# Layer 1's attention: half of the loads of the last keys' values issued one tile later, and the third bank's exponentials after the fourth query product

## What is computed

```python
x = x + tanh(g_xattn[0]) * L0_xattn(layernorm(x), ctx)      # 16 heads of 16
x = x + tanh(g_ffn[0])   * L0_ffn(layernorm(x))             # mixture of 8 experts, tokens 0..1023
x = x + tanh(g_xattn[1]) * L1_xattn(layernorm(x), ctx)      # 16 heads of 64, 77 keys
x = x + tanh(g_ffn[1])   * L1_ffn(x)                        # 32 prototypes, the two nearest, rank 16
```

```python
q = x @ Wq / 8 ; logits = q k^T ; w = softmax(logits) ; ctx = w v ; y = x + gate * ctx @ Wo
dist to 32 prototypes -> two nearest, weights wt ; y += gate * sum_t wt * (A[idx] @ (B[idx] @ y) + bias[idx])
```

## Time and profile before

| | |
|---|---|
| runs shown | 3024.16, 3027.03, 3029.62 us; median 3027.03 |
| profiled execution | 3032.24 us, with a span of 3030.5 us |
| granted TensorE clock over the span | 0.97 |
| busy share of the span | PE 91%, DVE 81%, ACT 73%, POOL 69% |
| stage of layer 1 | from about 1450 us to the end |
| its bodies 4 to 15, 16 to 47, 48 to 61 | 1547 to 1837, 1837 to 2595, 2595 to 2920 us |

### The profile page before, as it was taken

How to read it: one execution, slowest core, us unless ns; L and a number is a source line. 1 busy time by engine, 2 the same in 40 slices (tenths; PEclk the granted TensorE clock), 3 DMA queues, 4 the chain that set the end, 5 groups by cost and what they waited for, 6 DMA issues and landing times. The chain is left out here.

```text
span 3030.5 us, 96782 instructions
## 1 busy us (share of the span) xinstructions
PE 2744.3 (91%) x31534; PEld 2165.7 (71%) x31534; DVE 2452.0 (81%) x5870; ACT 2202.5 (73%) x5452; POOL 2090.0 (69%) x2777
## 2 busy tenths in 40 slices
PE   3889896899999999789699999999999999999996
PEld 2444444677777777557588878888878888888884
DVE  6888786688888888675588898888888888888884
ACT  2666666677787777575577777788777788778873
POOL 3893000566667666554478888888888888888886
PEclk7999999899999999899899999999999999999998
DMA  5997666223323233632467677777767777777763
GB/s 152 352 346 292 244 255 254 78 77 91 84 80 93 77 90 85 219 111 48 110 142 157 150 153 150 145 147 144 145 139 152 147 146 145 155 148 149 151 132 75
DMA packets 636894, 455.53 MB, mean 150 GB/s; under 512 B 387712, under 2 KB 610544, under 8 KB 631600
## 3 DMA queue, kind: packets, MB, share of 16 engines
q1 hardware_dynamic: 616240, 402.30, 53.7%
q0 software_dynamic: 7328, 23.40, 2.5%
q10 hardware_dynamic: 12960, 25.23, 2.3%
HBM read 235.08 MB, written 148.83 MB: 127 GB/s over the span
## 5 line engine op out<-in xcount | busy, mean ns | idle before, releaser
L383 POOL TENSOR_TENSOR a_probT_lo<-a_expT,a_probT_hi 128x512 f16<-128x512 f32 x256 | 291.4, 1159 | 217.7 <-ACT a_probT_hi L466 217.7
L459 ACT ACTIVATE a_expT<-banks,a_top,w_score_scale 128x512 f32<-128x512 f32 (+1 forms) x384 | 272.6, 710 | 152.8 <-PE banks L550 145.3
L1160 POOL TENSOR_TENSOR a_pn<-a_prob,a_rsum 128x1024 f32<-128x1024 f32 (+1 forms) x256 | 310.6, 1235 | 54.1 <-DVE a_rsum L1541 54.0
L1242 ACT ACTIVATE a_qT_hi<-banks 128x512 f16<-128x512 f32 x252 | 151.2, 600 | 212.3 <-PE banks L152 212.3
L150 PE MATMUL banks<-a_xnT,w_q_hi 128*128 128x256 f16 x1024 | 280.6, 274 | 15.4 <-DMA a_xnT<-a_xn_parts 13.5
L150 PE MATMUL banks<-a_vo_front,a_probT_hi 128*128 128x256 f16 x1024 | 279.9, 273 | 9.0 <-DVE a_probT_lo L1527 3.5
L1525 DVE TENSOR_TENSOR a_qT_lo<-banks,a_qT_hi 128x512 f16<-128x512 f32 x252 | 172.4, 684 | 141.6 <-ACT a_qT_hi L1242 141.6
L151 PE MATMUL banks<-a_xnT,w_q_hi 128*128 128x256 f16 x1024 | 280.3, 274 | 0.0
L152 PE MATMUL banks<-a_xnT,w_q_lo 128*128 128x256 f16 x1024 | 280.2, 274 | 0.0
L152 PE MATMUL banks<-a_vo_front,a_probT_lo 128*128 128x256 f16 x1024 | 279.9, 273 | 0.0
L151 PE MATMUL banks<-a_vo_front,a_probT_hi 128*128 128x256 f16 x1024 | 279.8, 273 | 0.0
(11 more groups left out here) (383 smaller groups left out, 10323.8 us busy)
## 6 DMA issues: line engine op xcount, KB each, us to landing
vo<-kv_vo_out SPq DMA_DIRECT2D x38, 2048.0 KB, 7.4
a_vo_front<-vo SPq DMA_DIRECT2D x128, 512.0 KB
kt<-kv_k_out ACTq DMA_DIRECT2D x9, 2560.0 KB, 15.0
a_k<-kt SPq DMA_DIRECT2D x64, 308.0 KB, 3.9
kv_raw_e<-in_L_ffn_w POOLq DMA_DIRECT2D x16, 1024.0 KB, 9.7
a_x<-in_x SPq DMA_DIRECT2D x64, 256.0 KB
a_y<-in_x SPq DMA_DIRECT2D x64, 256.0 KB, 2.8
x<-a_y SPq DMA_DIRECT2D x64, 256.0 KB, 3.0
```

Source lines behind the costliest of these rows:

```text
L383: pool.tensor_tensor(probT[b][1][:, first:end, :], expT[b][:, first:end, :], probT[b][0][:, first:end, :], ALU.subtract).then_inc(prob_rea ...
L459: act.activation(expT[1 - h][0:rows, first:end, :], bank, ACT.Exp, bias=top[0:rows, 0:1], scale=weights["score_scale"][0:rows, 0:1]).then_ ...
L1160: last = pool.tensor_tensor(keys_of(pn[h]), e[:, :, first:end], rsum[h][:, :].unsqueeze(2).broadcast_to([P, H, end - first]), ALU.mult)
L1242: act.activation(out, bank[:, 0:cols].rearrange("p (c s) -> p c s", c=out.shape[1]), ACT.Copy, scale=scale)\
```

## The change

`load_values` gets a range of the eight `vo_back` loads. In half 0 SP issues the two `vo_front` loads and the first four `vo_back` loads; in half 1, after the store of the output, it issues the other four. They then stand ahead of the next body's keys and `xnT`. And in ScalarE's list `prep(4)`, the high part of the fourth query product, comes ahead of `third_exponentials`; `prep(4)` has work in half 1 alone.

```diff
-        def load_values(i, u, j):
+        def load_values(i, u, j, first, end):
             p, _ = turn(u, j, 2)
             need(sp, y_ready, (i - 1) * TPB)
-            for a in range(2):
+            for a in range(2 if first == 0 else 0):
                 sp.dma_start(vo_front[p][a * FRONT:(a + 1) * FRONT, :, :, :], values_front(batch_at(i), a)).then_inc(vo_in[p], 16)
-            for n in range(MAIN):
+            for n in range(first, end):
                 sp.dma_start(vo_back[p][n * BACK:(n + 1) * BACK, :, :, :], values_back(batch_at(i), n)).then_inc(vo_in[p], 16)
...
-                if h == 0 and live(i, NB):
-                    load_values(i, u, j)
+                if live(i, NB):
+                    load_values(i, u, j, *((0, MAIN // 2), (MAIN // 2, MAIN))[h])
...
+                prep(4)
                 if live(t, NT):
                     third_exponentials(t, u, h)
-                prep(4)
                 prep(2)
```

## The result

The changed kernel takes 3105.5 us (median of 4 runs, 3101.4 to 3110.0) against 3028.3 us for the kernel before (4 runs). The ratio is 1.026, with a 95% interval of 1.025 to 1.028: slower by 77 us, where 31 were forecast, and outside the range given. The profiled execution took 3101.4 us with a span of 3099.7, 69.2 us more than before. The 77 us are the difference of the medians; the profiled execution before lay 4 us above its median, and this one was the fastest of its four.

A forecast was written before the change was run, and what follows sets the result against it. The prediction took TensorE's list to bound the kernel. Its terms, 29 + 9 + 1 - 8 - 0 = 31 us, put the time at 3058 us by the median of 3027.0, with a range of 3022 to 3080.

The forecast's parts named there:

- What bounds the kernel: TensorE's list sets the time; the change can win only from its idle pieces, 32.0 + 8.9 us and 17.0 us.
- Part 1, what it relieves: With four loads instead of eight on SP, `hwT` goes out when ready, 2.9 us earlier; gain 8 us, bounds 0 and 12.7.
- The term of 8 us: Gain taken in the loop's bodies from `hwT` going out when ready; bounds 0 and 12.7 us.
- Part 1, what it delays: Four loads ahead of the next body's `xnT` make TensorE wait: 29 us loop, 1 us last stretch, 9 us first stretch.
- the loop's sum: In the loop `xnT` is issued about 2009.9, lands at 2013.9, wanted at 2012.87; 0.9 us wait taken, 29 us in 32 bodies.
- 1 us in all: Last stretch: wait for `xnT` of 0.1 us in 14 bodies, bounds 0 and 14 us.
- The first stretch's 9 us: Wait for `xnT` of 1.5 us in six bodies with the experts' rows, 9 us, bounds 3 and 14.
- A landing of 4.8 us everywhere: Rival, 0.08: small loads slow the transpose; waits of 32 x 1.8 + 14 + 14 = 86 us, less 8: 3105 us.
- Part 2: ScalarE exchange: VectorE's stall moves to a wait for `attend`, `a_pick` still ends with GpSimd's L1167; 0 us, otherwise 9 us.
- the transpose lands in time: Rival, 0.12: at the first query product TensorE never waits for `xnT`; 3019 us, or 3014 with 12.7 us won.
- delay and gain even out: Rival, 0.07: waits of 0.1 to 0.4 us in the loop and 3 us in the first stretch, 3025 to 3033 us.
- the selections slip past GpSimd: Rival, 0.08: VectorE gets both `a_pick` in before L1167; idle time at `low` vanishes in 46 bodies, -28 us, giving 3030 us.

## Why the prediction was wrong in size

*What bounds the kernel* held. TensorE's list sets the time, its idle pieces were nearly all there was to win, and a new wait was paid in full: the three stretches have 68.9 us of waits for `xnT` and are 75.8 us longer.

*Part 1, what it relieves.* `hwT` did go out in time, and its gain was hidden by VectorE's low part, as the argument from the earlier trace rows had it. The term of 8 us looks too large: the loop of the run with two late loads won 0.9 us, together with 3.9 us of new waits, so some 5 us. That is one execution of each, and whole executions of one kernel differ by more than this.

*Part 1, what it delays*, is the step that failed, in its size. The mechanism was right, and the terms of the loop's sum were near. Counted from the end of `attend`, `xnT` was to be issued at 6.5 us and to land 4.0 us later. Over all 32 bodies of the changed kernel, issue was at 6.9 us and landing 4.2 us later on average, so 11.1 where 10.5 was worked out and 10.4 taken. With 9.5 wanted that is 1.6 us late, not 0.9. The waits listed show 1.37 us of it: a matmul is recorded for 0.27 us and the next follows after 0.11, so the idle time listed begins 0.16 us after TensorE could have gone on. Three choices made the sum too small:

- I worked out 1.0 us and took 0.9, with the argument that a store less stood ahead of the transpose. The landing did not get shorter: its median in the loop is 4.0 us, as before, and its mean 0.2 us more than the 4.0 taken. With an issue 0.4 us later than forecast that makes some 0.6 us in each of 32 bodies, and the 0.1 us makes it 0.7. The 44.0 us listed, with 32 times 0.16 us, are 49 us, where 29 were forecast.
- In the last stretch I took the loop's 4.0 us for the landing and found the transpose just in time, 1 us in all. It was 11.8 us. The issue came as forecast, 5.6 us after the end of `attend`; but these 14 transposes, which landed in 3.8 us in the median before, now took 4.7, nearly the bound of 4.8 for which the prediction says 14 us. With the loads alone they took 4.2 in the median, and the wait was 10.8 us. The changed kernel's lines on keys and transpose in the last stretch, with us to landing at the end, and the transpose's line in the run with two late loads:

```profile
a_k<-kt SPq DMA_DIRECT2D x14, 308.0 KB, 3.5
...
a_xnT<-a_xn_parts SPq DMA_TRANSPOSE x14, 4.7
...
a_xnT<-a_xn_parts SPq DMA_TRANSPOSE x14, 4.1
```

- The first stretch's 9 us were 13.1. They stood in six bodies, those with the experts' rows, as forecast, but at 2.2 us each instead of 1.5.

In the last stretch the keys were issued some 1.7 us ahead of `xnT` before, and are 0.7 us ahead now, since SP no longer waits for the rows to be ready between them. That the 308 KB right ahead make the landing longer can be part of it at most. With two late loads the keys are just as close, 0.7 us ahead, and none of the 14 transposes took 5 us; in the changed kernel seven did, 5.0 to 5.6 us. No run took the keys away, so what makes those seven long isn't shown.

*A term was missing*: what a wait does to the clock. In a body of the changed kernel's loop, these windows stand before and behind the first query product, which starts at 1908.96:

```profile
1906.96:1908.96 2.00, 0.00 (x1) 0.01 (x1) 1.59 (x6) 0.00 (x0) 1.92 (x4) 1.00 0.73 197
1908.96:1909.70 0.74, 0.74 (x7) 0.67 (x8) 0.00 (x0) 0.00 (x0) 0.58 (x2) 1.00 1.09 344
1909.70:1913.00 3.30, 3.30 (x18) 2.29 (x17) 1.29 (x6) 0.60 (x1) 1.31 (x2) 0.50 1.10 188
```

TensorE was idle for 2.00 us, ran seven matmuls at the full level, and then 3.3 us at a granted 0.50, the 1.2 GHz level. At the full level the 24 matmuls of the first two query products take 2.6 us; here 4.3. Four bodies of the loop show it, 1.7 us each, and two of the first stretch. I had looked at TensorE's clock only for whether it was high, not for what an idle piece beside it would do.

The kernel before had shown it already, in the loop whose mean clock of 0.99 I read as high. Three of its idle pieces there, two waits for `hwT` of 2.26 and 1.75 us and one of 1.88 us at 2218 for nothing that the profile shows, were followed by these windows of it:

```profile
1959.42:1962.83 3.41, 3.41 (x18) 2.33 (x16) 3.37 (x11) 1.20 (x4) 3.41 (x6) 0.50 1.13 271
2171.05:2174.46 3.41, 3.41 (x18) 2.38 (x16) 3.38 (x8) 2.00 (x6) 3.41 (x4) 0.50 1.12 233
2218.83:2225.66 6.83, 5.77 (x68) 4.29 (x67) 2.79 (x7) 4.34 (x13) 4.02 (x3) 0.50 0.54 87
```

So the change's waits for `xnT` lowered the clock in four bodies of the loop, and it took away the waits for `hwT` that had lowered it in two. The third piece has its like in the changed kernel, 2.04 us at 2255, and the clock stayed high there. TensorE was busy at 0.50 for 12.6 us of the loop before and for 13.7 us after: the loop lost almost nothing by it. The first stretch had none before and has 9.1 us after. As half of such time is lost, the clock accounts for about 5 of the 75.8 us, nearly all of it in the first stretch.

The stretches' growth then adds up as 68.9 us of waits for `xnT`, 4.2 us less of all other idle time, and 11.1 us more busy time: 75.8 us. Of the busy time 5.1 us are the clock. The other 6.0 us fit with 37 more idle pieces (140 before, 177 after) at 0.16 us each, the tail of the matmul recorded before each of them. My sum had 39 - 8.

*The range.* A landing of 4.8 us everywhere was a rival at 3105 us, which is where the kernel landed, and I gave it 0.08 and cut the range below it. It got there by another mixture: 4.2 us on average in the loop, 4.7 after it, a later issue, and the clock in the first stretch. That the time agrees with this rival's is luck. The bounds of the single terms, 14 us each for the two outer stretches, held for the waits; the range did not reach to them.

*Part 2* was right, in its result and in its mechanism: 0 us, the stall moved to a wait for `attend`, and the selections ended with GpSimd's line 1167. The run with the exchange alone shows both. By the rule that the Trainium skill states in "SBUF — State Buffer", section "SBUF: two separate sides", the shared port pair is locked for a whole instruction, and the traces agree: VectorE came 0.09 us sooner and ended 0.04 us after GpSimd's instruction, as it did before, and a pair with no GpSimd instruction beside it took 0.51 us instead of 1.62. That the pair's end goes with GpSimd's and not with its own start is shown by that. That the lock is the cause isn't shown by a run, as none moved GpSimd's instruction away.

*The rivals.* That the transpose lands in time is out for four loads, and true in most bodies for two. That delay and gain even out is out with it. That the selections slip past GpSimd is out: the pair got longer by what VectorE came sooner.

What stays open: what makes the transpose's landing longer in the last stretch, and whether a kernel without GpSimd's instruction beside the selections would win the 0.6 to 0.8 us per body that now hide the gains on the transposes. No run answers either. The exchange with two late loads (3025 us) isn't told from the kernel before.

## What to carry to other kernels

When loads are moved in an in-order queue, the price is not theirs but that of the most urgent transfer behind them: write down when each one behind is issued, how long it takes to land and when it is wanted, and treat the slack, here 1.5 us, as the number of loads that may pass, here one or two of 0.99 us. Where a landing time is borrowed from other surroundings, let the range reach to its bound in every stretch at once. Before a wait is costed as the idle time alone, look at what the engine's clock does after it, and after the waits that the change takes away.

## What the runs showed of the hardware that was not expected

After waits of TensorE of about 2 us and more the granted clock fell to 0.50 in many bodies, but not in all: of nine waits of 1.95 us or more for `xnT` in the changed kernel's loop, four were followed by it and five were not (2.01, 1.97, 2.09, 2.11 and 2.29 us). With six late loads, 29 of 32 bodies of the loop had it, for up to 6.0 us, and the mean clock of the loop fell from 0.99 to 0.92. In the kernel before, an idle piece of 1.75 us was enough once.

The DMA transpose's landing time in otherwise equal bodies varied between 3.3 and 5.5 us in the changed kernel's loop, with the same DMAs around it in the same order.
